# One attention projection moved behind the first expert tile's turns and up products, and one semaphore for each of two row stores

## The chip, the cores and the metric

The kernel runs on one core of one Trainium2 chip. The metric is the device time of one execution in microseconds; the time before is the median of three runs.

## The reference

Eight sequences of 512 tokens with 256 channels are normalised; the result goes through a windowed attention and through a top-2 mixture of eight experts, and both are added to the input.

```python
# x: (8, 512, 256)
xn = layernorm(x)
# attention: 16 heads of 16, windows of 128 tokens with stride 64; of the windows' rows,
# laid one after the other, the first 512 are used: four windows per sequence
qkv = xn @ w_qkv + b_qkv
ow = softmax(q_window @ k_window.T / sqrt(16)) @ v_window
attn = (ow as rows)[:, :512] @ w_out + b_out
# experts: E = 8, hidden width 512
probs, idx = softmax(top_k(xn @ gate_w.T, 2))
h1, h2 = split(xn @ w12[e].T)
expert_out = (silu(h1) * h2) @ w3[e].T
out = x + attn + sum(probs * expert_out)
```

## The kernel before

The program is written by hand as five instruction streams (TensorE, VectorE, ScalarE, GpSimd, and SyncE, which only issues transfers); each stream runs in its own order, and semaphores tie them together. There is no planner: the order of the text is the order of each engine.

It goes in four parts. First come the normalisation, the gate scores and the turned tokens. Then batches 0 and 1 of the attention run (`EXTRA` = 2), while the rows are sorted to expert tiles. Then comes the expert loop, 71 tiles of 128 rows (`SLOT_TILES`), each with the weights of one expert. Last come attention batches 2 to 7, with the final sums and the stores. The change is at the border of the second and the third part.

**The end of an attention window.** Each batch has four windows, each in two units. When a window's weighted sums are complete in PSUM, ScalarE copies the sums to `SIDE` and the softmax denominators to `DENS` (`sides`, L760 and L761). VectorE inverts `DENS` (`invert`, L1062). GpSimd multiplies both into `OTS` (`divide`, L574). TensorE multiplies `OTS` by the output weights into bank 7 (`project`, 4 matmul records). VectorE adds the bias and writes the rows to `XN` (`project` of the vector stream), which raises `r_free`. The denominators lie in the last 256 columns of the space of `XN`.

**The rows of batches 0 and 1.** They wait in `XN` for the end of the kernel, but the expert loop needs their space, so SyncE stores them to `rows_scratch`, one transfer per batch (`keep`, L464, 512 KB each). The transfer of batch 1 is issued when the last projection of batch 1 has been added.

**The split weights.** For a tile, ScalarE copies a half (512 columns times two chunks) of the expert's up weights to `WS` in a rounded form (`high_part`, L829), and VectorE writes the rest, the weights less that copy (`low_part`, L350). `WS` lies over the space of `XN`, and has two buffers. Tile 0 uses the second one: its low half 1 lies over `DENS`. Tile 1 uses the first: its high half 0 lies over the rows of batch 0 and its low half 0 over the rows of batch 1. The address of the weights is read from a list into a register first (`weights_of`, L343), in the stream of the engine that uses it.

**The first tiles.** `tokens(j, k)` turns the gathered rows of tile j (L1428); ScalarE and VectorE split the turned rows (L849 `take_xt`, and `low_xt`, L897 with output `XTS`). `up(j, k, half)` makes 6 products of 512 columns (L1206, `PS<-WS,XTS`): half 0 is the part that goes through the activation, half 1 the factor. It waits for `low_ready[half]`, and half 0 also for `xt_free`. `turn_hidden` (L1450) and `down` follow. Ahead of all of it TensorE waits, among others, for the last projection's completion (`r_full`), for the freed attention banks and for `weights_in`, the load of all expert weights; ScalarE waits for `weights_in` ahead of `high_part(0, 0, 0)` (L834).

Before the change the streams read at this place:

```python
# TensorE:  project() of batch 1's last window, waits, tokens(0,0), tokens(1,1), up(0,0,0), up(0,0,1), loop
# VectorE:  invert, project, low_part(0,0,0), wait r_free, low_xt(0,0), low_xt(1,1),
#           low_part(0,0,1), low_part(1,1,0), hidden(0,0), low_part(1,1,1), loop
# ScalarE:  high_part(0,0,0), high_part(0,0,1), take_xt(0,0), take_xt(1,1),
#           wait rows_out >= 32 (both stores), high_part(1,1,0), take_tanh(0,0), high_part(1,1,1), loop
# SyncE:    keep(0), load_tokens(2), keep(1), wait for both stores, wait for the expert loop's end
```

`hidden(j, k)` is two VectorE steps (L1172, L897 with output `WORK`) that make the hidden rows of tile j from its two halves.

Of the kernel before, what the change touches and what calls it, by code (L numbers as in the profile page):

```python
# [32 lines left out]
NWIN = L // WIN  # L33
# [18 lines left out]
LAST = B - 1  # L52
MAP_UNIT = 2
EXTRA = 2
# [43 lines left out]
def layer(nc, x, wqkv, bqk, bv, wout, bout, gate, wexp, out):  # L98
    with ExitStack() as ctx:
# [8 lines left out]
        def sem(name):  # L108
            return ctx.enter_context(nc.semaphore(name))
# [13 lines left out]
        XN = sb("XN", [P, NT, D])  # L123
# [182 lines left out]
        r_full, r_free = sem("r_full"), sem("r_free")  # L306
# [7 lines left out]
        y_stored = sem("y_stored")  # L314
        xs_in = [sem("xs_in0"), sem("xs_in1")]
        xt_full, xt_high, xt_free = sem("xt_full"), sem("xt_high"), sem("xt_free")
        rows_out = sem("rows_out")
        high_ready = [sem("high_ready0"), sem("high_ready1")]
        low_ready = [sem("low_ready0"), sem("low_ready1")]
        h1_full, tanh_ready, g_done = sem("h1_full"), sem("tanh_ready"), sem("g_done")  # L320
# [34 lines left out]
        def _(sp):  # L355
# [105 lines left out]
            def keep(b):  # L461
                sp.wait_ge(r_free, (b + 1) * NWIN + 1)
                t = slice(b * TB, (b + 1) * TB)
                sp.dma_start(rv[:, t, :], XN[:, t, :]).then_inc(rows_out, 16)  # L464

            begin(0)
            load_experts(FIRST_EXPERTS, EARLY)
# [6 lines left out]
            keep(0)  # L474
            load_tokens(2)
            keep(1)
            sp.wait_ge(rows_out, 16 * EXTRA)
            sp.wait_ge(y_stored, 1)

            def send_later(n, b):  # L480
# [187 lines left out]
        def _(act):  # L668
# [146 lines left out]
            for stage in range(2):  # L815
                if stage == 0:
                    for b in range(EXTRA):
                        batch(b)
                    take_shift(EXTRA % 2, 1)
                else:  # L820
                    for b in range(EXTRA, B):
                        batch(b)
                    break
                def high_part(j, k, half, used=None):

                    weights = weights_of(act, j, half)
                    if used is not None:
                        act.wait_ge((h1_full, h2_full)[half], used)
                    act.activation(WS[:, 1 - k, half, 0], weights, ACT.Copy  # L829
                                   ).then_inc(high_ready[half], 1)  # L830

                act.wait_ge(temps_done, 1)
                act.wait_ge(weights_in, 16 * E * CHUNKS)
                act.wait_ge(map_done, 1)  # L834
                high_part(0, 0, 0)
                high_part(0, 0, 1)
                act.wait_ge(probs_ready, c["ST"].now() + 2)

                def take_tanh(j, k):
                    act.wait_ge(h1_full, j + 1)  # L840
                    act.activation(HID[:, k, :], bank(2 * k), ACT.Tanh, scale=0.5).then_inc(tanh_ready, 1)

                def take_ht(j):
                    act.wait_ge(ht_full, j + 1)
                    act.activation(HTS, bank(6).rearrange("p (c n) -> p c n", c=FC), ACT.Copy).then_inc(ht_free, 1)  # L845

                def take_xt(j, k):
                    act.wait_ge(xt_full, j + 1)
                    act.activation(XTS[:, k, 0], bank(4 + k)[:, 0:D].rearrange("p (c n) -> p c n", c=NC_D),  # L849
                                   ACT.Copy).then_inc(xt_high, 1)  # L850

                def take_y(j, k, stored):
                    act.wait_ge(y_full, j + 1)
                    wait_some(act, y_out[k], 16 * stored)
                    act.activation(YS[k], bank(7)[:, 0:D], ACT.Copy).then_inc(ys_ready, 1)  # L855

                take_xt(0, 0)
                take_xt(1, 1)
                act.wait_ge(rows_out, 16 * EXTRA)
                high_part(1, 1, 0)  # L860
                take_tanh(0, 0)
                high_part(1, 1, 1)
                def tile(j, k, i):
                    high_part(j + 2, k, 0, j + 1)
                    take_tanh(j + 1, 1 - k)
                    take_ht(j)
                    high_part(j + 2, k, 1, j + 1)
                    take_xt(j + 2, k)
                    take_y(j, k, i)

                tile(0, 0, 0)
                tile(1, 1, 0)
                with act.Fori(1, SLOT_TILES // 2) as i:
                    for k in range(2):
                        tile(2 * i + k, k, i)
                last = SLOT_TILES - 1
                take_ht(last)
                take_y(last, last % 2, last // 2)
                act.wait_ge(ht_free, SLOT_TILES + 1)
                act.wait_ge(ys_ready, SLOT_TILES + 1)  # L880
                act.wait_ge(high_ready[1], XS_TILES)
                act.sem_inc(phase_done, 1)
                act.wait_ge(phase_done, 3)
# [3 lines left out]
        def _(dve):  # L887
# [170 lines left out]
            def invert():  # L1058

                n = c["O"].add()  # L1060
                dve.wait_ge(sides_ready, 2 * n)
                dve.reciprocal(out=DENS, in_=DENS).then_inc(recip_ready, 1)  # L1062

            def project(b, n):
                t = b * TB + n
                total = BOUT[:] if b < OWN else XR[:, t, :]
                if b >= OWN:
                    dve.wait_ge(own_ready, (b - OWN) * TB + n + 1)
                dve.wait_ge(r_full, c["R"].add())
                tt(XN[:, t, :], R_BANK[:, 0:D], total, ALU.add).then_inc(r_free, 1)  # L1070
# [38 lines left out]
            def batch(b, first=None):  # L1109
                last = b == LAST  # L1110
                pending = b and not ends(b - 1)
                for u in range(UNITS):
                    if b == EXTRA and u == 0:
                        dve.wait_ge(y_stored, 1)
                    if not last and u < 4:
                        split(u)
                    if not (last and u >= UNITS - 3):
                        take_max()
                    if u in (2, 4, 6) or (u == 0 and pending):
                        invert()  # L1120
                    if first == 0:
                        if u == 0:
                            route(1)
                        if u == 2:
                            take_ranks()
                            bases()
                        if u == 3:
                            experts_of_tiles()
                            shares()
                        if u == 4:  # L1130
                            dve.wait_ge(tiles_ready, 2)
                        if u >= 4:
                            tags(u - 4)
                        if u == UNITS - 1:
                            tags(4)
                    if first == 1:
                        if u < 2:
                            tags(5 + u)
                        if u == 0:
                            places()  # L1140
                        if u == 1:
                            tags(7)
                        if u == MAP_UNIT:
                            take_map()
                        if u == MAP_UNIT + 1:
                            finish_map()
                    if b == 0 and u == 3:
                        dve.wait_ge(xn_out, 64)
                    if u == 1 and pending:
                        project(b - 1, NWIN - 1)  # L1150
                    if u % 2 == 1 and u > 1:
                        project(b, u // 2 - 1)
                if not last:
                    c["W"].add(NWIN)
                if ends(b):
                    invert()
                    project(b, NWIN - 1)

            for stage in range(2):
# [5 lines left out]
                        batch(b)  # L1165
                    break
                low_part(dve, 0, 0, 0)
                dve.wait_ge(r_free, c["R"].now() + 1)

                def hidden(j, k):  # L1170
                    dve.wait_ge(tanh_ready, j + 1)
# [6 lines left out]
                def low_xt(j, k):  # L1178
                    dve.wait_ge(xt_high, j + 1)
                    tt(XTS[:, k, 1], bank(4 + k)[:, 0:D].rearrange("p (c n) -> p c n", c=NC_D),  # L1180
                       XTS[:, k, 0].bitcast(F32), ALU.subtract).then_inc(xt_free, 1)

                low_xt(0, 0)
                low_xt(1, 1)
                low_part(dve, 0, 0, 1)
                low_part(dve, 1, 1, 0)
                hidden(0, 0)
                low_part(dve, 1, 1, 1)
# [13 lines left out]
        def _(pe):  # L1202
# [165 lines left out]
                last.then_inc(map_full, 1)  # L1368

            def batch(b, first=None):  # L1370
                par, last, ends = b % 2, b == LAST, b in (EXTRA - 1, LAST)
                for u in range(UNITS):
                    if not last:
                        if u == 0:
# [26 lines left out]
                        pe.wait_ge(map_taken, 1)  # L1401
                    if u % 2 == 1 and (u > 1 or (b and b != EXTRA)):
                        project()
                if ends:
                    project()

            for stage in range(2):
# [57 lines left out]
                tokens(0, 0)  # L1465
                tokens(1, 1)
                up(0, 0, 0)
                up(0, 0, 1)
                pe.wait_ge(r_free, c["R"].now() + 1)
                with pe.Fori(0, SLOT_TILES // 2) as i:  # L1470
# [56 lines left out]
```

## Time and profile before

| | |
|---|---|
| median of 3 runs | 756.08 us (755.24 to 756.56) |
| the profiled execution's own time | 756.35 us |
| its span (first to last instruction) | 754.6 us |
| TensorE, VectorE, ScalarE, GpSimd busy | 666.5, 572.2, 505.3, 298.0 us |
| mean granted clock of TensorE | 0.973 of full speed |
| the expert loop | about 177 to 552 us of the span |
| the attention after it | from about 555.6 us |

All times of the rows are microseconds from the start of the span. A clock of 1.00 is 2.4 GHz, 0.50 is 1.2 GHz. The engine "ACTq" or "DVEq" means the instruction queue of that engine, where it reads registers and waits for semaphores. "PE", "DVE", "ACT", "POOL" and "SP" are TensorE, VectorE, ScalarE, GpSimd and SyncE.

### The profile page before, as it was taken

To read this page: it belongs to the slowest core of one execution; us is meant where nothing else is said; L and a number is where in the kernel's file an instruction comes from. 1 tells how busy PE (TensorE), PEld (TensorE's weight loads), DVE (VectorE), ACT (ScalarE), POOL (GpSimd) and SP (SyncE) were. 2 spreads that over 40 slices of the span, in tenths; PEclk is the share of its full clock that TensorE was granted. 3 is DMA by queue.
4 is the path that set the end of the run, shared out by engine and by line. 5 is a ranking of instruction groups with operands and counts; after the bars stand their busy time and mean duration, and the time that the engine had idled before them with its cause. 6 is when DMAs were issued, how large, how long until landed. Compare 5 with 4: busy or idle time off the path is not lost.

```text
span 754.6 us, 17174 instructions
## 1 busy us (share of the span) xinstructions
PE 666.5 (88%) x5648; PEld 516.6 (68%) x5649; DVE 572.2 (76%) x907; ACT 505.3 (67%) x880; POOL 298.0 (39%) x329
## 2 busy tenths in 40 slices
PE   0766676879999999999999999999989998999984
PEld 0554454657778878787877877888857676766663
DVE  4856898967877777777777787777758879797883
ACT  4534477476676767676766667676756788888884
POOL 3000173032444545444444544454411235566553
PEclk9996989998999999999999999999999999999998
DMA  8597493481111111111111111111136787875830
GB/s 285 186 298 239 109 335 109 124 286 40 49 49 49 49 48 49 49 56 42 50 47 56 49 49 49 49 49 49 49 106 199 198 256 189 277 197 178 223 110 29
DMA packets 66303, 92.56 MB, mean 123 GB/s; under 512 B 6384, under 2 KB 53360, under 8 KB 66256
## 3 DMA queue, kind: packets, MB, share of 16 engines
q1 hardware_dynamic: 57248, 68.83, 30.3%
q0 software_dynamic: 6864, 18.75, 7.9%
q10 hardware_dynamic: 2144, 4.34, 1.8%
q8 instruction: 31, 0.51, 0.3%
q14 instruction: 16, 0.13, 0.1%
HBM read 59.06 MB, written 32.83 MB: 122 GB/s over the span
## 4 chain that ended last, share of the span: by engine, by line
PE 62%; DVE 13%; ACT 8%; issue 7%; DMA 6%; POOL 2%; SPq 1%; ACTq 0%; POOLq 0%; DVEq 0%
PE PS L1206 56%; PE PS L1450 4%; DVE SMALL L903 3%; ACT WORK L753 3%; PE PS L1428 2%; DVE XN L1062 2%; DMA KS<-parts_scratch 2%; DVE WALL L897 2%; DMA XN<-in_x 1%; ACT QS L748 1%; DMA parts_scratch<-WORK 1%; DVE WORK L972 1%; DMA WORK<-xt_scratch 1%; DVE WORK L965 1%; DVE WALL L921 1%
## 5 line engine op out<-in xcount | busy, mean ns | idle before, releaser
L350 DVE TENSOR_TENSOR WS<-WALL,WS 128x1024 fp32r<-128x1024 f32 x144 | 176.4, 1226 | 90.0 <-ACT WS L829 88.8
L1206 PE MATMUL PS<-WS,XTS 128*128 128x512 f32 x852 | 235.6, 412 | 2.0 <-DVE XTS L897 1.5
L1206 PEld LDWEIGHTS PS<-WS,XTS 128*128 128x128 f32 x852 | 151.1, 190 | 46.3 <-DVE XTS L897 14.1
L829 ACT ACTIVATE WS<-WALL 128x1024 fp32r x144 | 152.2, 1059 | 39.3 <-issue 36.4
L1206 PE MATMUL PS<-WALL,WORK 128*128 x568 | 136.1, 382 | 0.8 <-ACT WORK L845 0.8
L574 POOL TENSOR_TENSOR OTS<-SIDE,XN 128x256 f32<-128x256 f32 x32 | 24.2, 755 | 221.9 <-DVE XN L1062 147.3
L1206 PEld LDWEIGHTS PS<-WALL,WORK 128*128 128x128 f32 x568 | 102.2, 190 | 12.8 <-issue 1.0
L633 POOL DMA_INDIRECT WORK<-xn_scratch,WORK x72 | 100.9, 1402 | 23.8 <-issue 21.6
L903 DVE TENSOR_REDUCE SMALL<-PS 128x8 f32<-128x1024 f32 x64 | 77.4, 1210 | 20.9 <-PE PS L1206 19.8
L637 POOL DMA_INDIRECT ys_scratch<-SIDE,WORK x36 | 41.9, 1163 | 117.8 <-ACT SIDE L855 117.8
L753 ACT ACTIVATE WORK<-PS 128x512 f32<-128x512 f32 x128 | 69.4, 595 | 23.3 <-PE PS L1206 19.9
L748 ACT ACTIVATE QS<-PS 16x1024 bf16<-16x1024 bf16 x64 | 65.0, 1016 | 12.9 <-PE PS L1302 11.3
L637 POOL DMA_INDIRECT ys_scratch<-OTS,WORK x35 | 34.6, 989 | 71.1 <-ACT OTS L855 71.1
L1206 PEld LDWEIGHTS PS<-KS,QS 96*128 96x128 bf16 x512 | 34.0, 103 | 38.4 <-DVE SMALL L903 23.3
L1206 PE MATMUL PS<-KS,QS 96*128 96x128 bf16 x512 | 42.4, 229 | 18.4 <-DVE SMALL L903 11.0
L1062 DVE RECIPROCAL XN<-XN 128x256 f32<-128x256 f32 x32 | 55.9, 1746 | 0.0
L897 DVE TENSOR_TENSOR WORK<-WORK,PS 128x512 f32<-128x512 f32 x71 | 48.8, 687 | 2.5
L1172 DVE SCALAR_TENSOR_TENSOR WORK<-WORK,PS 128x512 f32<-128x512 f32 x71 | 48.3, 680 | 0.0
L1206 PE MATMUL PS<-WORK,WQKV 128*128 128x320 f32 x112 | 40.3, 486 | 8.6 <-DMA WORK<-xt_scratch 4.1
L1206 PE MATMUL PS<-WOUT,OTS 128*128 128x256 f32 x128 | 37.1, 413 | 12.1 <-POOL OTS L574 11.4
L1206 PE MATMUL PS<-WORK,VW 128*32 128x128 f32 x1024 | 42.2, 283 | 5.2 <-ACT WORK L753 5.2
L1206 PE MATMUL PS<-QS,KS 112*128 112x128 bf16 x512 | 40.5, 223 | 5.2 <-ACT QS L748 5.2
(137 smaller groups left out, 971.6 us busy)
## 6 DMA issues: line engine op xcount, KB each, us to landing
WALL<-in_wexp SPq DMA_DIRECT2D x24, 384.0 KB
WALL<-ys_scratch SPq DMA_DIRECT2D x16, 512.0 KB, 7.0
parts_scratch<-WORK SPq DMA_DIRECT2D x32, 240.0 KB, 2.5
QS<-parts_scratch SPq DMA_DIRECT2D x16, 480.0 KB, 4.6
XN<-in_x SPq DMA_DIRECT2D x4, 1024.0 KB, 12.3
xn_scratch<-XN SPq DMA_DIRECT2D x4, 1024.0 KB, 8.9
WALL<-in_x SPq DMA_DIRECT2D x8, 512.0 KB, 5.6
KS<-parts_scratch SPq DMA_DIRECT2D x16, 240.0 KB, 3.9
```

The costliest lines, as they stand in the source:

```text
L350: eng.tensor_tensor(out=WS[:, 1 - k, half, 1], in0=weights, in1=WS[:, 1 - k, half, 0].bitcast(F32), op=ALU.subtract).then_inc(low_ready[ha ...
L633: pool.indirect_dma_start(XS[:, j % 2, :], None, xn_dram, bass.IndirectOffsetOnAxis(GIDX[:, j:j + 1], 0)).then_inc(xs_in[j % 2], 16)
L637: pool.indirect_dma_start(ys_dram, bass.IndirectOffsetOnAxis(SIDX[:, j:j + 1], 0), YS[j % 2], None).then_inc(y_out[j % 2], 16)
L748: act.activation(to, SHIFT_ROW.unsqueeze(1).to_broadcast([2 * HH, HH, WIN]), ACT.Copy).then_inc(t_free, 1)
L753: act.activation(PT[:, 2 * (u % 2) + q, :], ST_BANK[q], ACT.Exp, scale=SCALE).then_inc(probs_ready, 1)
L829: act.activation(WS[:, 1 - k, half, 0], weights, ACT.Copy).then_inc(high_ready[half], 1)
L897: return dve.tensor_tensor(out=o, in0=a, in1=b, op=op)
L903: return dve.tensor_reduce(out=o, in_=a, axis=AX_X, op=op, **kw)
L1062: dve.reciprocal(out=DENS, in_=DENS).then_inc(recip_ready, 1)
L1172: dve.scalar_tensor_tensor(out=HID[:, k, :], in0=HID[:, k, :], scalar=1.0, in1=bank(2 * k), op0=ALU.add, op1=ALU.mult).then_inc(g_done, 1)
L1206: return pe.matmul(o, a, b, start=start, stop=stop)
L1450: last = pe.transpose(bank(6)[:, f * P:(f + 1) * P], HID[:, k, f * P:(f + 1) * P], IDF[:])
```

## The change

- **One semaphore for each store of early rows.** `rows_out` becomes a list; ScalarE waits only for the store of batch 0 ahead of `high_part(1,1,0)`. VectorE gets a new wait, for the store of batch 1, ahead of `low_part(1,1,0)`. SyncE waits for both, as before.
- **TensorE.** The last `project()` of batch 1 goes behind `tokens(0,0)`, `tokens(1,1)` and `up(0,0,0)`, and ahead of `up(0,0,1)`.
- **VectorE.** The addition that belongs to it goes behind `low_part(0,0,0)`, `low_xt(0,0)` and `low_xt(1,1)`, ahead of `low_part(0,0,1)`, and the wait for `r_free` moves with it. The inversion stays where it was.

```diff
-        rows_out = sem("rows_out")
+        rows_out = [sem(f"rows_out{b}") for b in range(EXTRA)]
@@ SyncE
-                sp.dma_start(rv[:, t, :], XN[:, t, :]).then_inc(rows_out, 16)
+                sp.dma_start(rv[:, t, :], XN[:, t, :]).then_inc(rows_out[b], 16)
...
-            sp.wait_ge(rows_out, 16 * EXTRA)
+            for b in range(EXTRA):
+                sp.wait_ge(rows_out[b], 16)
@@ ScalarE
                 take_xt(1, 1)
-                act.wait_ge(rows_out, 16 * EXTRA)
+                act.wait_ge(rows_out[0], 16)
                 high_part(1, 1, 0)
@@ VectorE, batch
                 if ends(b):
                     invert()
+                if last:
                     project(b, NWIN - 1)
@@ VectorE, ahead of the expert loop
                 low_part(dve, 0, 0, 0)
-                dve.wait_ge(r_free, c["R"].now() + 1)
...
                 low_xt(0, 0)
                 low_xt(1, 1)
+                project(EXTRA - 1, NWIN - 1)
+                dve.wait_ge(r_free, c["R"].now() + 1)
                 low_part(dve, 0, 0, 1)
+                dve.wait_ge(rows_out[1], 16)
                 low_part(dve, 1, 1, 0)
@@ TensorE, batch
-                par, last, ends = b % 2, b == LAST, b in (EXTRA - 1, LAST)
+                par, last = b % 2, b == LAST
...
-                if ends:
+                if last:
                     project()
@@ TensorE, ahead of the expert loop
                 tokens(1, 1)
                 up(0, 0, 0)
+                project()
                 up(0, 0, 1)
```

## Rows read from the trace of the kernel before

**Rows 1.** The page: busy time by engine, and the granted clock in 40 slices.

```profile
PE 666.5 (88%) x5648; PEld 516.6 (68%) x5649; DVE 572.2 (76%) x907; ACT 505.3 (67%) x880; POOL 298.0 (39%) x329
...
PEclk9996989998999999999999999999999999999998
```

**Rows 2.** Chain that ended last, 180 to 545 us: shares by engine and line.

```profile
by line: PE PS L1206 87.7%; PE PS L1450 8.3%; PE PS L1428 4.1%
```

**Rows 3.** Chain that ended last at the border: start, length, what.

```profile
163.38 1.67 DVE XN L1062
...
165.18 0.73 POOL OTS L574
...
165.95 1.15 PE PS L1206 x4
...
167.12 0.44 DVE XN L897
...
167.57 3.67 DMA rows_scratch<-XN
...
171.90 1.06 ACT WS L829
...
173.10 1.23 DVE WS L350
...
174.96 0.32 DVE WORK L897
...
175.73 1.24 DVE WS L350
...
177.01 1.66 PE PS L1206 x6
```

**Rows 4.** ScalarE's queue at L834, the wait for all expert weights: count, ns, start.

```profile
L834 ACTq EVENT_SEMAPHORE  x1: 3282/3282/3282, 162.2 to 162.2; - x1
```

**Rows 5.** Timeline of ScalarE: start, length, instruction, idle before it.

```profile
166.36 2.00 ACT L829 ACTIVATE WS<-WALL 128x1024 fp32r x2 [1.91 <-issue]
168.39 0.66 ACT L849 ACTIVATE XTS<-PS 128x256 fp32r<-128x256 f32 x2
171.90 1.06 ACT L829 ACTIVATE WS<-WALL 128x1024 fp32r x1 [2.85 <-DMA rows_scratch<-XN]
```

**Rows 6.** Timeline of VectorE, same columns.

```profile
168.17 1.23 DVE L350 TENSOR_TENSOR WS<-WALL,WS 128x1024 fp32r<-128x1024 f32 x1 [0.62 <-issue]
169.31 0.75 DVE L897 TENSOR_TENSOR XTS<-PS,XTS 128x256 fp32r<-128x256 f32 x2
```

**Rows 7.** Timeline of TensorE, same columns.

```profile
167.14 1.10 PE L1428 MATMUL PS<-IDF,WORK 128*128 128x128 f32 x4
169.78 6.36 PE L1206 MATMUL PS<-WS,XTS 128*128 128x512 f32 x18 [1.53 <-DVE XTS L897]
...
177.01 1.20 PE L1206 MATMUL PS<-WS,XTS 128*128 128x512 f32 x4 [0.42 <-DVE WS L350]
```

**Rows 8.** Groups of TensorE instructions that start from 169.7 to 174 us.

```profile
L1206 PE MATMUL PS<-WS,XTS 128*128 128x512 f32 x10 | 4.5, 632 | 1.5 <-DVE XTS L897 1.5
```

**Rows 9.** Stretches: length, busy of each engine, granted clock, DMA share, GB/s.

```profile
163.00:167.00 4.00, 1.05 (x4) 0.68 (x4) 2.04 (x2) 2.07 (x3) 0.72 (x1) 1.00 0.70 260
167.30:174.00 6.70, 5.17 (x14) 3.90 (x15) 4.26 (x6) 3.82 (x7) 1.93 (x2) 0.50 0.38 120
174.10:178.00 3.90, 3.48 (x17) 2.68 (x16) 3.79 (x5) 3.11 (x5) 0.00 (x0) 1.00 0.00 0
```

**Rows 10.** DMA share in tenths, 163 to 168 us in 40 slices.

```profile
DMA  9999999999999998996434322110010000000000
```

**Rows 11.** Chain in the expert loop, at full clock.

```profile
187.28 0.44 PE PS L1450 x4
187.71 1.40 PE PS L1206 x6
```

**Rows 12.** Chain at the kernel's end, clock 0.50: the last projection.

```profile
748.65 2.09 PE PS L1206 x4
```

## The prediction

> **What bounds the kernel now.** I read the page first: TensorE is busy for 88% of the span, and its clock is at full speed in nearly every slice [rows 1]. The chain of work that ended last, cut to 180 to 545 us, is then TensorE alone, line after line without a wait [rows 2]. So the expert loop has no slack on TensorE: whatever moves its start moves its end by the same amount, and the attention behind it starts only at the loop's end. The question is at what time the loop gets going.
>
> The same chain cut to 163 to 177 us shows what sets that start [rows 3]. The reader should follow it as a relay: inversion 163.38, division 165.18, last projection 165.95, its addition 167.12 to 167.56, the store of batch 1's rows 167.57 to 171.24, ScalarE's high part for tile 1 at 171.90, VectorE's low part at 173.10, then hidden (the chain's 174.96 is its last step), the next low part 175.73 to 176.96, and the second half of tile 1's up products at 177.01. TensorE's own row there has 0.42 us of idle time, released by VectorE's low part [rows 7]. So the loop starts behind the store.
>
> Three neighbours matter. ScalarE's queue stood at the wait for all expert weights for 3.28 us from 162.2, so until 165.45 [rows 4]; its two high parts for tile 0 end at 168.36 and the two copies of turned rows start at 168.39 [rows 5]. None of these hangs on the last projection. VectorE's low part for tile 0 started at 168.17 and the split of the turned rows at 169.31 [rows 6]; TensorE began the up products at 169.78 on that split [rows 7].
>
> **Parts that help.** TensorE's turns go ahead of the projection. They still wait for the weights, 165.45, so they run from about 165.8 instead of 167.14; this buys nothing by itself, since ScalarE can't copy the turned rows before 168.39 [rows 5]. On VectorE the addition no longer stands ahead of the low part. The high part it needs ends 1.06 us after 166.36, at 167.42, so the low part runs from about 167.55 to 168.8 instead of from 168.17. The first copy of turned rows is there at about 168.78 (0.38 us, half of the pair with their overlap, after 168.39), the first split ends about 0.43 us after its start at 168.84, and the up products start at 169.30 instead of 169.78: **0.48 us earlier**. ScalarE no longer waits for batch 1's store. The store of batch 0 has to land before 169.06, and the transfers have drained by 167 [rows 10], so its high part for tile 1 runs at about 169.7 instead of 171.90, beside TensorE. GpSimd has no instruction moved; its next gather starts some 1.3 us earlier with the turns and is hidden.
>
> **Parts that cost.** The projection now stands behind up(0,0,0) on TensorE. The clock decides its time. It was at 1.00 up to 167.0, at 0.50 from 167.3 to 174.0, and at 1.00 again after; in the stretch ahead of the fall TensorE was busy 1.05 us of 4.00 [rows 9]. With the projection's work taken out of that stretch and the turns put in, TensorE is no busier, so I let the clock fall as before.
>
> - Up products at half clock: ten of the 18 [rows 7] start between 169.78 and 174.0 [rows 8], so 0.42 us each; six take 2.55 us. From 169.30 they are issued by 171.85.
> - The projection at half clock: the last projection of the kernel ran at 0.50 and took 2.09 us [rows 12], against 1.15 us at full clock [rows 3]. It ends at 173.94.
> - The addition: 0.44 us and a gap of 0.02 [rows 3], so `r_free` comes at 174.40. Before it came at 167.56: **6.84 us later**.
> - The store: nothing else stands ahead of it on SyncE, and it is issued at once, as before: 3.67 us plus 0.02 to its issue [rows 3]. It lands at 178.09. Behind it on SyncE stand only waits for the loop's end.
> - VectorE's low part (1,1,0) now waits for this itself, with hidden(0,0), low part (1,1,1) and all of the loop queued behind it. The reading of the weights' address stands behind the wait too: 0.77 us, as from the product at 174.96 to the low part at 175.73 [rows 3]. It starts at **178.86**. Before it started at 173.10, after the store at 171.24, ScalarE's address and copy and its own start. So of the chain 171.24 to 173.10 (1.86 us) only 0.77 is left, a gain of 1.09; the later `r_free` costs 6.84; with rounding the net is **5.76 us later**.
>
> Low part (0,0,1) is moved as well: it starts 0.77 us after 174.40, at 175.2, and ends at 176.4. TensorE, done with the projection at 173.94, waits for it with up(0,0,1), then has 1.4 us of work at full clock or 2.6 at half, and waits for low part (1,1,0) until 178.86 + 1.25 = 180.11. Both are hidden under the store.
>
> From there VectorE's relay is as before: hidden and the next low part end 5.76 us later, 176.96 + 5.76 = 182.72. TensorE has its own sum for the same point. Between 174.0 and 180.1 it works 1.4 to 2.6 us of 6.1, a share near that which stood ahead of the last fall [rows 9], so I put it at half clock at 180.11. Six products 2.55 us, four turns twice their 0.44 us [rows 11], ends 183.54. That is later than 182.72, so TensorE is the bound again, **6.53 us** behind 177.01. In the trace of before the clock came back 4.2 us after the products began without a break (169.78 to 174.0); the same from 180.11 gives 184.3, so some 0.8 us more of work at half clock, which loses half of it, 0.4. Sum: 6.53 + 0.4 = **6.9 us later**.
>
> The phase of the clock is the choice in this. The lower bound with the clock at full speed at 180.1 is VectorE's 5.76. If the clock comes back 3 us later than I put it, 1.5 us more is lost: 8.4. The Trainium skill (TensorE: Matmul & The Clock Gate, Part 1) says that the slow clock is the default and activity lifts it, after a time and not after a number of matmuls, and that this differs from run to run with the phase. The trace agrees in that the clock rose in the middle of an unbroken series, at 174.0. By that rule the 0.4 us could be any value from 0 to the 1.5 above, and the forecast stays a middle one.
>
> The sum against the profiled execution's own time: 756.35 + 6.9 = 763.25. That execution was 0.27 us above the median; against the median it is 763.0.
>
> **Rivals.** About 0.2% (1.5 us) is what a measurement of this kernel can tell from no change.
>
> - *The slow clock doesn't strike twice, or not at all* (slower by 3.7 to 5.7). If TensorE were at full speed from 169.30: six products 1.40 [rows 11], projection 1.15 [rows 3], so 171.85; `r_free` 172.31; store lands 176.00; low part 176.77. That is 3.67 us later than 173.10, and 759.8 us. For it: the turns and the projection no longer follow each other at the fall. Against it: the clock fell in this place with more work in the stretch than there will be [rows 9]. Chance 0.17, most of it near 5.7.
> - *The other side: the new wait is found passed.* Then only the 0.48 us earlier start is left, 755.6 us (with ScalarE's earlier high part possibly another 0.5 us). For it: ScalarE stood idle for 2.85 us until the second store had landed [rows 5], though its next copy needs only the first. The deciding point: batch 1's rows would have to have landed by 172.3, so that low part (1,1,0) can start at 173.1 after reading its address. That needs `r_free` by 168.6, while the projection stands behind products that start at 169.3. Even a transfer of no length wouldn't do: 174.40 + 0.77 is 175.2. Chance 0.03.
> - *The delay is absorbed later.* The expert loop would have to wait for something that isn't moved. The chain has none in 365 us [rows 2]. The one loss at the end that depends on clock phase is the last projection, 2.09 us instead of 1.15, so 0.9 us could come back. That makes 6.0 of 6.9 and not zero. Chance of no difference 0.03.
> - *More is lost* (over 8.4): a third slow stretch, or a store that takes 4.5 us or more. Chance 0.05.
>
> **How the numbers follow.** The forecast, slower by 5.7 to 8.4, has 0.72: alone it would give 761.8 to 764.5. With the first rival (0.17) the range reaches down to 759.5. At the top 764.8 leaves out only the last case. Slower by more than 0.2%: 0.72 + 0.17 + 0.05 = 0.94; within: 0.03; faster: 0.03.
>
> **What would show it.** In the trace after: up products from about 169.3; the projection's four records behind the sixth; VectorE's addition near 174; the store of batch 1's rows issued near 174.4 and landed near 178; ScalarE's high part for tile 1 ahead of 171; a VectorE idle time of 2 us or more ahead of low part (1,1,0) that ends with `rows_scratch<-XN`; a slow clock in 178 to 184; the second half of tile 1's up products at 182.7 to 184. From there the loop should run as before and take the same 375 us. I would be wrong if VectorE's addition came ahead of 169, if the low part didn't wait for the store, or if the loop got shorter.

## The result and the profile after

The changed kernel takes 760.68 us (median of 7 runs, 759.17 to 763.03) against 755.67 us before (7 runs); the ratio is 1.0073 with a 95% interval of 1.0054 to 1.0092. It is slower by 5.5 us, with an interval of 4.1 to 7.0. The profiled execution took 759.91 us, its span is 758.2 us.

The chain that ended last in the changed kernel, at the border of the attention and the expert loop (start, length, what; it answers to [rows 3]). Its first line is one of the transfers of the weights; the whole load had landed only at 163.6, as ScalarE's row further down shows:

```profile
154.84 7.34 DMA WALL<-in_wexp
162.18 0.49 ACT WORK L754
...
164.53 1.07 ACT WS L830
...
165.73 1.22 DVE WS L350
...
166.97 0.44 DVE XTS L898
...
167.45 4.65 PE PS L1210 x10
172.10 0.02 issue
172.12 0.44 DVE XN L898
172.56 0.02 issue
172.58 2.91 DMA rows_scratch<-XN
175.49 0.03 issue
...
176.27 1.24 DVE WS L350
177.51 0.04 issue
177.55 2.93 PE PS L1210 x6
180.48 0.85 PE PS L1454 x4
181.33 1.97 PE PS L1210 x6
```

The relay has new members. The inversion and the division are gone from it: they are hidden behind the load of the weights. But the six up products and the projection now form one piece, 10 records in 4.65 us, ahead of the addition, and the store comes behind them. VectorE's low part (1,1,0) at 176.27 hangs on that store directly. The reader should also see that two more TensorE pieces stand between the store and the loop, and that they are long: 2.93 us for six products that take 1.40 us in the loop, and 0.85 us for four turns that take 0.44 [rows 11].

VectorE's timeline (start, length, instruction, idle time before it and what ended it; it answers to [rows 6]) shows the two waits, one for TensorE and one for the store:

```profile
162.22 0.42 DVE L898 TENSOR_TENSOR XN<-PS,BOUT 128x256 f32<-128x256 f32 x1 [1.08 <-PE PS L1210]
...
172.12 0.42 DVE L898 TENSOR_TENSOR XN<-PS,BOUT 128x256 f32<-128x256 f32 x1 [4.39 <-PE PS L1210]
173.36 1.23 DVE L350 TENSOR_TENSOR WS<-WALL,WS 128x1024 fp32r<-128x1024 f32 x1 [0.81 <-DVE XN L898]
176.27 1.23 DVE L350 TENSOR_TENSOR WS<-WALL,WS 128x1024 fp32r<-128x1024 f32 x1 [1.68 <-DMA rows_scratch<-XN]
```

The stretches of the span (length, busy of each engine, granted clock, DMA share, GB/s; they answer to [rows 9]) show two slow stretches where there was one:

```profile
161.00:165.30 4.30, 1.81 (x9) 1.10 (x8) 2.23 (x3) 3.34 (x6) 0.72 (x1) 1.00 0.92 343
165.50:172.10 6.60, 4.63 (x10) 3.16 (x10) 1.98 (x3) 4.26 (x8) 1.97 (x2) 0.50 0.13 42
172.30:175.50 3.20, 0.86 (x4) 0.73 (x5) 1.48 (x2) 0.77 (x1) 0.00 (x0) 1.00 0.49 164
175.70:182.40 6.70, 5.90 (x16) 4.22 (x15) 5.47 (x6) 1.57 (x3) 0.00 (x0) 0.50 0.00 0
182.50:186.00 3.50, 3.50 (x18) 2.96 (x17) 2.25 (x3) 1.41 (x4) 0.04 (x1) 1.00 0.00 0
```

TensorE was at half clock from 165.5 to 172.1, came back, was busy for 0.86 of the next 3.20 us, and fell again until 182.4. What it waited for in those 3.20 us is VectorE's low part (0,0,1), which now stands behind the addition, and then low part (1,1,0):

```profile
174.64 2.11 PE L1210 MATMUL PS<-WS,XTS 128*128 128x512 f32 x6 [2.56 <-DVE WS L350]
177.55 2.93 PE L1210 MATMUL PS<-WS,XTS 128*128 128x512 f32 x6 [0.80 <-DVE WS L350]
```

ScalarE's queue stood at the wait for all expert weights (it answers to [rows 4]) for 2.19 us from 161.4, so until 163.6. Here and in [rows 4] the row carries the line of the last of three waits that follow each other (L834 before, L835 here). That it ended with the weights shows in their last landings, 163.59 here and 165.42 before:

```profile
L835 ACTq EVENT_SEMAPHORE  x1: 2192/2192/2192, 161.4 to 161.4; - x1
```

From there on the loop is as it was. The chain cut to 180 to 545 us answers to [rows 2]:

```profile
by line: PE PS L1210 87.7%; PE PS L1454 8.4%; PE PS L1432 4.1%
```

**Where the time went.** The two executions didn't reach the border at the same time: the addition of the second last window began at 162.22 in the changed kernel and at 162.96 before (VectorE's timeline of before: "162.96 0.42 DVE L897"). So I count from that addition, in microseconds:

| from the addition of the second last window to | before | after | later by | after, another execution | later by |
|---|---|---|---|---|---|
| first up products begin | 6.82 | 5.23 | -1.59 | 5.45 | -1.37 |
| last window's rows are in place (`r_free`) | 4.60 | 10.34 | 5.74 | 9.81 | 5.21 |
| VectorE's low part (1,1,0) begins | 10.14 | 14.05 | 3.91 | 13.51 | 3.37 |
| tile 1's second half begins | 14.05 | 19.11 | 5.06 | 17.42 | 3.37 |

Tile 1's second half itself then took 1.97 us, 0.57 us more than the 1.40 of the loop, since the clock was still low. That makes 5.6 us, against the 5.5 us of the ratio. The close match is luck in part. The last two columns are from the profiled execution of the changed kernel's second measurement, reported at the end of the experiments: the same mechanism, but only 3.4 us. So one trace gives the order of events, and its length only to within 1.7 us.

### The profile page after: what moved, and what is told of

Same layout as the page of the kernel before. It is cut to its first block, busy times and chain, and to the rows that moved or that the text cites. A ratio compares the mean times of both kernels' runs of the same rounds, so it can differ in the third digit from the quotient of the medians.

```text
span 758.2 us, 17173 instructions
## 1 busy us (share of the span) xinstructions
PE 669.8 (88%) x5648; PEld 519.4 (69%) x5649; DVE 572.4 (75%) x907; ACT 505.3 (67%) x880; POOL 298.2 (39%) x329
## 4 chain that ended last, share of the span: by engine, by line
PE 62%; DVE 12%; ACT 8%; issue 7%; DMA 6%; POOL 2%; SPq 1%; ACTq 0%; DVEq 0%; POOLq 0%
PE PS L1210 56%; PE PS L1454 4%; DVE SMALL L904 3%; ACT WORK L754 3%; PE PS L1432 2%; DVE XN L1063 2%; DVE WALL L898 2%; ACT QS L749 1%; DMA XN<-in_x 1%; DMA WORK<-xt_scratch 1%; DMA parts_scratch<-WORK 1%; DVE WORK L973 1%; DMA WALL<-in_wexp 1%; DVE WORK L966 1%; DMA KS<-parts_scratch 1%
## 5 line engine op out<-in xcount | busy, mean ns | idle before, releaser
L1210 PE MATMUL PS<-WS,XTS 128*128 128x512 f32 x852 | 238.0, 415 | 6.1 <-DVE WS L350 3.4
L754 ACT ACTIVATE WORK<-PS 128x512 f32<-128x512 f32 x128 | 69.4, 595 | 25.8 <-PE PS L1210 22.6
L842 ACT ACTIVATE WORK<-PS 128x512 f32<-128x512 f32 x71 | 41.2, 580 | 9.7 <-PE PS L1210 9.7
```

Of the source, the lines that this page charges most:

```text
L754: act.activation(PT[:, 2 * (u % 2) + q, :], ST_BANK[q], ACT.Exp, scale=SCALE).then_inc(probs_ready, 1)
L1210: return pe.matmul(o, a, b, start=start, stop=stop)
```

## The experiments

All ratios are to the kernel before, run on the same chip in the same rounds; kernels in different rows are best compared by them. I call the time from the addition of the second last window to the start of tile 1's second half the *lead*: 14.05 us before, 19.11 us in the changed kernel. It comes from one execution each. Outside it the traces differ too: for the kernels whose leads are given here, the stretch ahead of that addition by up to 3.5 us (161.64 to 165.13), the one behind the lead by up to 2.5 us (575.3 to 577.8). So a difference of a lead under 2 us says little by itself.

| kernel | median us | ratio | 95% interval |
|---|---|---|---|
| the changed kernel, first time | 760.68 | 1.0073 | 1.0054 to 1.0092 |
| the changed kernel, again | 760.20 | 1.0059 | 1.0038 to 1.0080 |
| semaphores only | 755.04 | 0.9992 | 0.9978 to 1.0005 |
| order only | 761.66 | 1.0087 | 1.0070 to 1.0103 |
| turns first | 755.44 | 1.0000 | 0.9985 to 1.0015 |
| changed, last rows through SIDE | 759.16 | 1.0052 | 1.0035 to 1.0069 |
| changed, many added products | 762.48 | 1.0095 | 1.0075 to 1.0115 |
| changed, half as many | 756.95 | 1.0027 | 1.0014 to 1.0040 |
| changed, SIDE and added products | 755.37 | 1.0009 | 0.9992 to 1.0027 |
| before, added products | 754.35 | 0.9978 | 0.9966 to 0.9990 |
| semaphores only, added products | 752.42 | 0.9966 | 0.9950 to 0.9981 |

**Semaphores only.** The diff's two semaphores, with the order of before.

```diff
# the order of before
-                act.wait_ge(rows_out, 16 * EXTRA)
+                act.wait_ge(rows_out[0], 16)
...
                 low_part(dve, 0, 0, 1)
+                dve.wait_ge(rows_out[1], 16)
                 low_part(dve, 1, 1, 0)
```

> The order of before, with one semaphore for each store: ScalarE waits for batch 0's rows only, VectorE for batch 1's rows ahead of low part (1,1,0). Theory (the expert loop starts behind the store of batch 1's rows, and the loss of the changed kernel is the later store, not the new wait): ScalarE's high part for tile 1 leaves the chain, VectorE's low part (1,1,0) starts 0.77 us after the store has landed instead of 1.86 us, so 1.1 us earlier; TensorE had only 0.42 us of idle time ahead of tile 1's second half, so the time falls by 0.4 us, to about 755.3. Rival (a VectorE that waits for a transfer itself is what costs): slower than before by 1 us or more.

No difference that can be measured, on the theory's side of it, and the rival's 1 us or more is out. VectorE's timeline shows that the new wait cost nothing here: the two low parts went through back to back.

```profile
169.79 2.41 DVE L350 TENSOR_TENSOR WS<-WALL,WS 128x1024 fp32r<-128x1024 f32 x2
173.07 0.69 DVE L1173 SCALAR_TENSOR_TENSOR WORK<-WORK,PS 128x512 f32<-128x512 f32 x1 [0.87 <-ACT WORK L842]
174.60 0.69 DVE L898 TENSOR_TENSOR WORK<-WORK,PS 128x512 f32<-128x512 f32 x1 [0.84 <-PE PS L1208]
```

So low part (1,1,0) began near 171.0, long ahead of what [rows 3] shows, and it bought nothing: the next steps waited for TensorE's products, which ran at half clock. The lead was 14.02 us (162.65 to 176.67), with no store in its chain. So TensorE's path at half clock took as long here as the store's path of [rows 3], 14.05, and taking the store out of the chain gained nothing.

**Order only.** The new order of TensorE and VectorE, one semaphore for both stores.

```diff
# the changed kernel, with the one semaphore of before
...
-                act.wait_ge(rows_out[0], 16)
+                act.wait_ge(rows_out, 16 * EXTRA)
...
-                dve.wait_ge(rows_out[1], 16)
                 low_part(dve, 1, 1, 0)
```

> The new order of TensorE and VectorE, but one semaphore for both stores, on which ScalarE waits as before; VectorE doesn't wait for the store itself. Theory: the late store is the loss, and ScalarE's address and high part stand behind it again: 1.1 us more than the changed kernel's 760.7, so 761.8. Rival (the loss comes from VectorE's new wait): back to 755 to 757.

761.66, as the theory had it; the rival's 755 to 757 is out. The loss is there without VectorE's new wait. The chain shows ScalarE's copy behind the store once more:

```profile
172.85 2.92 DMA rows_scratch<-XN
...
176.43 1.06 ACT WS L829
...
177.63 1.24 DVE WS L350
```

**Turns first.** The semaphores, and the projection behind the turns but ahead of the up products.

```diff
# the order of before with two semaphores
-                if ends:
+                if last:
                     project()
...
                 tokens(1, 1)
+                project()
                 up(0, 0, 0)
```

> One part of the change alone: the order of before and the two semaphores, but the last projection stands behind the turns of tiles 0 and 1 (and ahead of the up products); VectorE as before. Theory: the turns wait for the weights as the projection waits for the division, at nearly the same time, so the result comes 0 to 0.9 us later than before: 755.0 to 756.3, and the loss of the changed kernel comes with the up products ahead of the projection. Rival (any step ahead of the projection costs what the change costs): 758 or more.

755.44, ratio 1.0000, and the rival's 758 is out. The turns ahead of the projection cost nothing and buy nothing. What costs is the projection behind the six products, and with it the addition behind VectorE's low part and splits; these two were moved together only, but in the changed kernel VectorE stood idle for 4.39 us until the projection was there. The profiled execution was the slowest of 12 (757.81 us). Its lead was 15.81 us (162.46 to 178.27), with TensorE at half clock from 165.7 to 175.8, where before it was 167.3 to 174.0.

**The last rows through SIDE.** In the changed kernel the last window's rows are added into `SIDE`, 128 rows of 256, and stored from there.

```diff
# the changed kernel, with a third semaphore in rows_out
...
-                sp.wait_ge(r_free, (b + 1) * NWIN + 1)
-                t = slice(b * TB, (b + 1) * TB)
+                sp.wait_ge(r_free, (b + 1) * NWIN + 1 - b)
+                t = slice(b * TB, (b + 1) * TB - b)
                 sp.dma_start(rv[:, t, :], XN[:, t, :]).then_inc(rows_out[b], 16)
+                if b:
+                    sp.wait_ge(r_free, (b + 1) * NWIN + 1)
+                    sp.dma_start(rv[:, (b + 1) * TB - 1, :], SIDE[:]).then_inc(rows_out[EXTRA], 16)
...
-                tt(XN[:, t, :], R_BANK[:, 0:D], total, ALU.add).then_inc(r_free, 1)
+                o = SIDE[:] if t == EXTRA * TB - 1 else XN[:, t, :]
+                tt(o, R_BANK[:, 0:D], total, ALU.add).then_inc(r_free, 1)
# ScalarE waits for the third semaphore ahead of its first copy of results into SIDE
```

> The changed kernel, but the last window's 128 rows of batch 1 are added into the buffer SIDE and stored from there; the other three windows' rows are stored as soon as they are there, and VectorE waits for those only. ScalarE waits for the store from SIDE ahead of its first result copy into SIDE. So the store's landing leaves the chain, while the projection still stands behind the first up products. Theory: VectorE's low part (1,1,0) follows low part (0,0,1) at once, about 1.5 us earlier than in the changed kernel (174.8 instead of 176.3): 759.2, still 3.5 us slower than before, since the projection on TensorE at half clock and the addition ahead of VectorE's low parts remain. Rival (the store's wait is the whole loss): 755.5.

759.16, where 759.2 stood, and the rival's 755.5 is out. So the store's landing isn't the whole loss. Its own share is at the edge of what these runs can tell: 1.0052 stands against 1.0073 and 1.0059 of the changed kernel, which is 0.5 to 1.6 us, and the intervals overlap. The theory's number came out, its 1.5 us share isn't shown. In this trace the lead wasn't shorter either (162.12 to 181.22, 19.10 us): TensorE was at half clock from 167.2 to 180.6. VectorE's row shows the low parts back to back, and still 4.40 us of idle time ahead of the addition:

```profile
172.69 0.42 DVE L903 TENSOR_TENSOR SIDE<-PS,BOUT 128x256 f32<-128x256 f32 x1 [4.40 <-PE PS L1216]
173.93 2.36 DVE L350 TENSOR_TENSOR WS<-WALL,WS 128x1024 fp32r<-128x1024 f32 x2 [0.81 <-DVE SIDE L903]
```

**Added products, too many.** Products of the identity into a bank that is free, to hold TensorE's clock.

```diff
# the changed kernel
                 pe.wait_ge(probs_ready, c["ST"].now() + 2)
+                for _ in range(16):
+                    mm(bank(6)[:, 0:P], IDF[:], IDF[:])
                 pe.wait_ge(weights_in, 16 * E * CHUNKS)
# likewise 20 behind tokens(1, 1), 16 behind project(), 12 behind up(0, 0, 1)
```

> The changed kernel with products of the identity into the free bank 6 in TensorE's idle times: 16 ahead of the wait for the weights, 20 behind the turns, 16 behind the projection, 12 behind up(0,0,1). They keep its clock at 1.00 and their results aren't used. Theory (about half of the loss is the slow clock): six up products 1.1 us and the projection 0.8 us shorter ahead of the store, then 1.2 us at tile 1's first half and 0.5 us in the remaining slow stretch: 3.2 to 3.6 us less than 760.7, so about 757.3. Rival (the clock plays no part): 760.7, or more if the added products delay something.

762.48: my theory missed by 5 us, through my arithmetic. TensorE's timeline tells why. The 16 products are 32 records in 3.81 us and the 20 are 40 in 4.63 us, about 0.22 us from one product to the next, where I had reckoned with the time of one record. The up products began at 172.61, with no idle time ahead of them, so 5 us later than in the changed kernel:

```profile
164.14 3.81 PE L1210 MATMUL PS<-IDF 128*128 128x128 f32 x32 [1.73 <-ACT QS L749]
167.78 0.60 PE L1434 MATMUL PS<-IDF,WORK 128*128 128x128 f32 x4
168.22 4.63 PE L1210 MATMUL PS<-IDF 128*128 128x128 f32 x40
172.61 1.64 PE L1210 MATMUL PS<-WS,XTS 128*128 128x512 f32 x6
```

This run doesn't tell the theory from the rival, but six products took 1.64 us instead of 2.93: the clock was held. A start 5 us later cost 2 us.

**Added products, about half as many.** 4, 10, 10 and 6.

> The changed kernel with half as many added products: 4 ahead of the wait for the weights, 10 behind the turns, 10 behind the projection, 6 behind up(0,0,1). In the run with the larger numbers such a product took 0.22 us and not the 0.11 us that I had reckoned, so there they stood in the way; these numbers are for idle times of 2.8, 2.5 and 1.5 us. Theory (part of the loss is the slow clock): with the clock at 1.00 throughout, the projection's result 1.9 us earlier, tile 1's second half bound by VectorE's low part and not by half-speed products: 757 to 758. Rival (the clock plays no part in the loss): 760.7.

756.95, just below the expected 757 to 758, and the rival's 760.7 is out. The clock's share of the loss is thus 2.4 to 3.5 us (1.0059 and 1.0073 less 1.0027). The lead was 17.46 us (162.48 to 179.94), and the clock was at 1.00 but for 164.3 to 167.4, at the turns. That is 1.65 us less than the 19.11 of the changed kernel's first trace, but the same as the 17.42 of its second: which part of the share lies in which step stays open. TensorE's timeline:

```profile
166.03 1.06 PE L1434 MATMUL PS<-IDF,WORK 128*128 128x128 f32 x4
166.88 2.72 PE L1210 MATMUL PS<-IDF 128*128 128x128 f32 x20
169.35 1.65 PE L1210 MATMUL PS<-WS,XTS 128*128 128x512 f32 x6
170.84 1.02 PE L1210 MATMUL PS<-WOUT,OTS 128*128 128x256 f32 x4
...
179.94 1.67 PE L1210 MATMUL PS<-WS,XTS 128*128 128x512 f32 x6 [0.51 <-DVE WS L350]
```

**Both remedies on the changed kernel.** SIDE, and 4, 10, 10 and 6 added products.

> The changed kernel with both remedies: the last window's rows go through SIDE, so that no weights wait for their store, and added products keep TensorE's clock at 1.00 (4, 10, 10 and 6 of them). Theory (the loss is the late store and the slow clock, on top of a projection and an addition that stand ahead of low part (0,0,1)): the 1.5 us of the one and about 3.5 us of the other add up, so 755.4 to 756, no difference from before; what is left to the 752.4 of the old order with the same clock is the place of the projection. Rival (the two overlap and the sum is smaller): 756.9, as with the clock alone.

755.37, ratio 1.0009 (0.9992 to 1.0027), just below the theory's 755.4 to 756. The changed kernel with both can't be told from the kernel before without either. That the two shares add up is likely and not shown: the clock alone had 1.0027, which is the upper end of this interval, so the rival isn't out. The step from there, 0.0018 or 1.4 us, is in the range of the 0.5 to 1.6 us that SIDE gave without the added products.

**Added products in the old order.** 12 ahead of the last projection, 8 behind the turns.

```diff
# the kernel before, and once more on top of the two semaphores
+                if b == EXTRA - 1:
+                    pe.wait_ge(w_free, c["W"].now() + 1)
+                    for _ in range(12):
+                        mm(bank(6)[:, 0:P], IDF[:], IDF[:])
                 if ends:
                     project()
...
                 tokens(1, 1)
+                for _ in range(8):
+                    mm(bank(6)[:, 0:P], IDF[:], IDF[:])
                 up(0, 0, 0)
```

> The kernel before with the same added products and nothing else. Theory: the chain goes through the store, ScalarE's copy and VectorE's low part, which don't depend on TensorE's clock, and TensorE had 0.42 us of idle time there: no difference that can be measured, 755 to 755.5. Rival (the slow clock sets the loop's start here as well): 1.5 us faster, 754.

754.35, ratio 0.9978 (0.9966 to 0.9990). The theory of no difference missed; the rival's 754 holds. The lead was 13.32 us (161.64 to 174.96), 0.73 less than before. The low part still waited for ScalarE's copy behind the store:

```profile
169.84 1.06 ACT L829 ACTIVATE WS<-WALL 128x1024 fp32r x1 [2.51 <-DMA rows_scratch<-XN]
```

But the store was issued at 166.25 and had landed at about 169.2, 2.9 to 3.0 us instead of the 3.67 of [rows 3], and that alone is the 0.73 us. If the store takes 2.9 us in ordinary executions of the kernel before, its path is the shorter one there and TensorE's half clock the bound. This agrees with the semaphores-only run, where the lead was 14.02 us without a store in its chain; but the traces of more executions of before would be needed to show it, so this stays an argument.

> The order of before with one semaphore for each store, and TensorE kept at full clock by 12 added products ahead of the last projection and 8 behind the turns. Theory: with ScalarE's copy out of the chain, the half clock from 167 to 174 us is what still holds tile 0's second half and so hidden(0,0): tile 1's second half starts near 175.0 instead of 176.7, so 1.6 us less than the 755.0 of the same order without added products: about 753.5. Rival (VectorE and ScalarE bind there anyway): 755.

752.42, ratio 0.9966 (0.9950 to 0.9981): the fastest of all, 2.6 us below the kernel before and 8 us below the changed one. The lead was 12.51 us (161.72 to 174.23), 1.5 us less than the 14.02 (162.65 to 176.67) of the semaphores alone, near the 1.6 forecast. It is a little over half of the 2.6 us; of the difference between these two executions 0.93 us lies ahead of the second last window's addition, where the kernels are the same. TensorE's timeline shows small gaps only:

```profile
164.72 1.13 PE L1208 MATMUL PS<-WOUT,OTS 128*128 128x256 f32 x4 [0.36 <-POOL OTS L575]
165.91 0.66 PE L1434 MATMUL PS<-IDF,WORK 128*128 128x128 f32 x4
166.40 1.95 PE L1208 MATMUL PS<-IDF 128*128 128x128 f32 x16
168.54 1.66 PE L1208 MATMUL PS<-WS,XTS 128*128 128x512 f32 x6 [0.20 <-DVE XTS L898]
```

With the clock held at nearly all of the border the two orders stand at 756.95 and 752.42, so the new order loses 4.5 us even there, with its store on the path. An order that wasn't tried is the changed one with low part (0,0,1) ahead of the addition, so that TensorE wouldn't wait 2.56 us for it.

**The changed kernel again.**

> The changed kernel once more on the same chip as the others, as their measure: 760.7 us, 0.7% slower than before, under every theory.

760.20, ratio 1.0059, in agreement with the first time. Its trace shows how much of the first one's account belongs to one execution. TensorE's timeline, and VectorE's wait for the store:

```profile
170.58 2.93 PE L1210 MATMUL PS<-WS,XTS 128*128 128x512 f32 x6 [2.33 <-DVE XTS L898]
173.31 1.15 PE L1210 MATMUL PS<-WOUT,OTS 128*128 128x256 f32 x4
177.01 4.78 PE L1210 MATMUL PS<-WS,XTS 128*128 128x512 f32 x12 [2.54 <-DVE WS L350]
...
182.55 1.66 PE L1210 MATMUL PS<-WS,XTS 128*128 128x512 f32 x6 [0.33 <-DVE WS L350]
...
178.64 1.23 DVE L350 TENSOR_TENSOR WS<-WALL,WS 128x1024 fp32r<-128x1024 f32 x1 [1.69 <-DMA rows_scratch<-XN]
```

The wait for the store is the same, 1.69 us. But the clock had come back by the time of the projection, which took 1.15 us, and its second slow stretch ended at 180.4, ahead of tile 1's second half:

```profile
177.10:180.30 3.20, 3.20 (x7) 2.10 (x8) 1.66 (x2) 0.00 (x0) 0.00 (x0) 0.50 0.09 31
180.50:184.00 3.50, 3.17 (x16) 2.40 (x15) 3.42 (x4) 2.15 (x3) 0.00 (x0) 1.00 0.00 0
```

TensorE waited 0.33 us for VectorE there, so VectorE was the bound and not the half clock, and the lead was 17.42 us (165.13 to 182.55), 3.37 more than before. This execution took 761.56 us all the same; its second last addition came 2.2 us later than before (165.13 against 162.96), ahead of anything that was changed.

## Why the prediction was right

It said 763.0 us, slower by 6.9; the median is 760.68, and the ratio says 5.5 us. The side and the mechanism were the ones forecast. The size was not quite: 5.5 us lies just below the main range of 5.7 to 8.4, in the wider one that goes down to 759.5. That part of the range was there for a clock that strikes once or not at all, and it struck twice; the number came out smaller for other reasons, earlier weights and a shorter store, which follow.

- **The loop has no slack, the start decides.** Right: the chain in the loop is TensorE alone again, with the shares of before, and the kernel ended later.
- **Up products 0.48 us earlier.** The direction held; counted from the same addition they were 1.59 us earlier. The 1.1 us on top is the weights: they had landed 2.49 us after that addition before (162.96 to 165.45) and 1.4 us after it in the changed kernel (162.22 to 163.6). Nothing of the change stands ahead of those loads. In the other traces the distance is 1.6 to 2.7 us, in both orders, so the spread of executions is the likely reason.
- **`r_free` 6.84 us later.** 5.74 us; the difference is the same 1.1 us. The piece in it, six products and the projection at half clock, was forecast at 4.64 us (2.55 + 2.09) and measured at 4.65. In the second trace it was 3.89, since the projection found the clock back.
- **The store, 3.67 us.** This term was mis-sized: 2.91 us in both traces of the changed kernel and 2.92 in the order-only run. I took a single row as the duration. The two gathers that ran beside it aren't the reason: in the semaphores-only run the store had them beside it as before, issued 0.4 and 1.7 us behind it, and took 2.94 us (167.26 to 170.20); in the run with the many added products it had none and took 3.71 us (175.61 to 179.32). Why one execution needs 2.9 and another 3.7 us stays open.
- **Low part (1,1,0) 0.77 us behind the landing.** 175.49 to 176.27 is 0.78. The match is luck in part: the 0.77 was 0.32 us of VectorE's last hidden step and 0.45 of reading the address, while here all 0.78 is the reading, whose first step alone took 0.31. It began 3.91 us later than before, where 5.76 stood: 1.1 from the weights and 0.75 from the store.
- **TensorE at half clock at 180 as the next bound.** Right in the first trace and not in the second. In the first the low part of the second half ended near 180.1, TensorE began it at 181.33. The clock was forecast to return at 184.3 and was back at 182.5; by then it had cost 0.57 us more, where 0.4 stood. In the second it was back at 180.4 and VectorE was the bound, near to the case of the prediction's lower bound of 5.76; with the shorter store (0.76), the earlier weights (0.9) and the faster projection (0.75) that comes to 3.35, where 3.37 was measured.
- **The rival of the fully held clock** was priced at 3.67 us, with the other terms of the prediction in it. The run with the added products lost 0.27% (0.14 to 0.40), 1.1 to 3.0 us, to the kernel before; its lead was 3.41 us longer than 14.05, with the clock at half for 164.3 to 167.4 of it.
- **The side on which it ends.** VectorE idled for 1.68 us for the store in spite of everything that helped. The rival "the new wait is found passed" came true only in the old order.
- **What I hadn't weighed in the kernel before:** that its own start is held by the half clock too. I read the 0.42 us of TensorE's idle time [rows 7] as a proof of the contrary. With the clock held and two semaphores the old order gains 0.34%, and without the clock held no difference could be measured.

So it is shown that the loss comes with the projection and its addition behind the six up products, and not with the semaphores or the turns. How it divides is shown only roughly: 2.4 to 3.5 us for the half clock, 0.5 to 1.6 us for the store's landing, and a rest that the combined run can't tell from nothing. Against the old order with its clock held that combined kernel is still 3 us slower (755.37 against 752.42). I take this for the place of the projection and of the addition ahead of VectorE's low parts; no run takes it apart.

## What to carry to other kernels

Filling an idle time with work pays only if nothing long hangs on the work that is moved back. Here the idle engine's 3 us were waited through anyway, for the weights, and the projection that lost its place was the head of a relay with a 3 us store at its end; look at what the moved step releases before you look at the gap it leaves. A gap at the border of two phases costs twice, once as idle time and once as half clock in the products behind it: a few products without use, counted by their time in the trace, gave more here than any new order (0.34% with the two semaphores). Where a buffer's last part holds up its reuse, one can put that part somewhere else, so that its store leaves the chain; here that was worth 0.5 to 1.6 us, at the edge of what could be measured. And a lead read from one trace is no more exact than its spread: two executions of the same kernel were 1.7 us apart.

## What the runs showed of the hardware

- TensorE's clock fell to 0.50 at the border, where it had been busy for 1.05 us of 4.00 in the kernel before [rows 9] and for 1.81 us of 4.30 in the changed one. With products of the identity in its idle times it stayed at 1.00, but for 164.3 to 167.4 us in one run. The gain was 0.22% of the whole kernel in the old order (0.9978) and 0.32 to 0.46% in the new one (1.0059 and 1.0073 against 1.0027).
- A product of the identity, 128 by 128 in f32, is two records and took 0.22 us in a row of 20 at full clock (40 records from 168.22 to the next product at 172.61), and not 0.11.
- The phase of the clock differed between two executions of the changed kernel: its second slow stretch at the border ended about 1 us after tile 1's second half had begun in one (182.4 against 181.33), and about 2 us ahead of it in the other (180.4 against 182.55).
- One transfer of 512 KB to DRAM took 2.91 to 2.94 us in five executions (both traces of the changed kernel, order only, semaphores only, half as many added products), 3.19 us with the turns first, and 3.67 and 3.71 us in the kernel before and with the many added products. Gathers beside it don't tell the two groups apart.
